# Graph network with four message layers: the collections' copies out of PSUM do part of the finishing, and statistics are taken by tile

## Chip, cores and metric

The program runs on one core of a Trainium2 chip. Its time is the device time of one execution in microseconds (us); of several executions the median is given.

## What is computed

Four message-passing layers (L = 0 to 3) run one after the other on 3125 nodes with 160 features each and 103125 edges. Each layer makes a message for each edge, sums the messages by target node, multiplies the sums by an output weight, finishes the row with node attribute, self-connection and gate, adds it to x and normalizes x over its 160 features. Cut to what the change touches (the sums over edges are `agg`, `scal`, `vec`, `ms`, `mv`):

```python
# layer 0
pre = self_connection + (agg @ lin2) * a * scale          # 192 columns
out = concat([silu(pre[:, :64]), sigmoid(pre[:, 64:96]) * pre_v])
# layer 1: returns x + attention output
# layer 2: mean over max(count, 1) edges
alpha = scal @ Wa * a * inv96
return sc + alpha * conv                                   # conv is also times a
# layer 3
angle = 0.1 * (ms @ W3) * a * inv96
return cos(angle) * sc + sin(angle) * (conv * a)
# after every layer
def _layernorm(x, axis=-1, eps=1e-05):
    m = jnp.mean(x, axis=axis, keepdims=True)
    v = jnp.var(x, axis=axis, keepdims=True)
    return (x - m) / jnp.sqrt(v + eps)
x = _layernorm(x + layer(x))
```

## The kernel before

Nodes are held in 25 tiles of 128 (n = `k.NT` = 25); `x` is one SBUF tile of 128 partitions by 25 by 160 numbers of 32 bits. Each layer is a row of phases, and each phase is a block in which every engine has its own program; between two phases all engines meet at a barrier (L139), so nothing of one phase overlaps the next. The phases of a layer are: `project` (rows of x times input weights, written to a table in memory), `messages` or the attention phases (most of the time, by groups of 512 edges), `collect`, and `finish`.

`collect` takes the sums per node (`acc`) and multiplies them by the output weight. For each of the 25 tiles TensorE (PE) transposes eight blocks of `acc` into `tp` (L430, L432), ScalarE (ACT) copies them to `st` and `st_rest` (L408 to L415), PE makes the product `po` with five matmuls (L442, L443), and VectorE (DVE) copies `po` out of PSUM to `out_all` (L468). `po` and `tp` have two slots each. PE starts the product of tile t+2 only when the copy of tile t is done (the semaphore `taken`, L439). In layer 1 DVE also divides `acc` by the softmax sums, one tile ahead of the transposes (L465), and PE waits for that (`scaled`, L428). The first two tiles and the last stand in straight code (in layer 1 the last three), the others in a loop that takes two tiles a round.

`hold` (L82) is a wait on a semaphore as an instruction of its own, which also counts up another semaphore. Inside the loop its value comes from a register, and so do the addresses `bass.ds(t, 1)`.

`finish` works on whole nodes, all 25 tiles in one instruction, 4000 numbers per partition: attribute and self-connection (L548, L549 in layer 0; L557, L558 in layer 1; L561 to L567 in layer 2; L570 to L594 in layer 3), then `layer_norm` (L485 to L493). Its instructions form a chain on DVE, each waiting for the one before (`link`). ACT is asked for silu, sigmoid, sine and square root (`ask`), each with a table load ahead of it. SP loads the next layer's input weights meanwhile (L270). `finish` ends before `project` starts.

Of the kernel before, what the change touches and what calls it, by code (L numbers as in the profile page):

```python
# [87 lines left out]
class Chain:  # L88
# [15 lines left out]
    def link(self, ins):  # L104
        self.need(self.run(ins))
# [268 lines left out]
                        v.sem_inc(drained)  # L374


def collect(nc, k, L, a, C, W, out_all, w, c):

    n = k.NT
    heads = L == 1  # L380
# [3 lines left out]
    with ExitStack() as scope:  # L384
# [9 lines left out]
        emptied = h.sem(name + "emptied")  # L394
        turned, staged, product, taken = (h.sem(name + "turned"), h.sem(name + "staged"), h.sem(name + "product"),
                                          h.sem(name + "taken"))
        with nc.Block() as block:

            @block.scalar
            def _(act):  # L400
                if not every:
                    act.wait_ge(emptied, 1)

                def step(t, s, i):
                    if not isinstance(t, int) or t >= 2:
                        hold(act, k, product, t - 1)
# [12 lines left out]
                rounds(act, n, step)  # L419

            @block.tensor
            def _(pe):
                def step(t, s, i):
                    if inside(t, n):
                        if not isinstance(t, int) or t >= 2:
                            pe.wait_ge(staged, t - 1)
                        if heads:
                            pe.wait_ge(scaled, t + 1)  # L428
                        for b in range(4):
                            pe.transpose(tp[:, s, 0, b * P:(b + 1) * P], acc[:, t * 4 + b, 0:P], k.ident[:, :])  # L430
                        for b in range(4):
                            mm = pe.transpose(tp[0:rest, s, 1, b * P:(b + 1) * P], acc[:, t * 4 + b, P:P + rest], k.ident[:, :])  # L432
                        mm.then_inc(turned, 1)
                    if inside(t - 1, n):
                        o = 1 - s
                        if isinstance(t, int) and t == 1:
                            pe.wait_ge(wready, 1)
                        if not isinstance(t, int) or t >= 3:
                            hold(pe, k, taken, t - 2)  # L439
                        pe.wait_ge(staged, t)  # L440
                        for y in range(4):
                            pe.matmul(po[:, o, 0:C], st[:, o, y, :, :].rearrange("p b n -> p (b n)"), w[:, y, :], start=y == 0, stop=False)  # L442
                        pe.matmul(po[:, o, 0:C], st_rest[:, o, :, :].rearrange("p b n -> p (b n)"), w[:, 4, :],  # L443
                                  start=False, stop=True).then_inc(product, 1)

                for t in range(n + 1):
                    step(t, t % 2, t // 2)

            @block.vector
            def _(v):  # L450
                chain = Chain(v, links)
                if not every:
                    chain.link(v.memset(st_rest[:, :, :, :], 0.0))
                    v.sem_inc(emptied)
                if heads:
                    chain.link(v.tensor_scalar(rden[:, :], acc[:, :, D], 1e-16, None, ALU.add))
                    chain.link(v.reciprocal(rden[:, :], rden[:, :]))
                else:
                    chain.link(v.tensor_tensor(w[:, :, :], w[:, :, :], c[:, :, :], ALU.mult))
                v.sem_inc(wready)  # L460

                def step(t, s, i):
                    if heads and inside(t + 2, n):
                        here = acc[:, bass.ds(t * 4 + 8, 4), 0:D]
                        v.tensor_tensor(here, here, over(rden[:, bass.ds(t * 4 + 8, 4)], 2, D), ALU.mult).then_inc(scaled, 1)  # L465
                    if inside(t, n):
                        hold(v, k, product, t + 1)
                        v.tensor_copy(out_all[:, bass.ds(t, 1), 0:C], po[:, s:s + 1, 0:C]).then_inc(taken, 1)  # L468

                rounds(v, n, step, before=2 if heads else 0)  # L470

# [7 lines left out]
    link(v.reciprocal(y, t))  # L479


def layer_norm(v, act_do, link, k, x, tmp, m, D_=D):

    n = x.shape[1]
    link(v.tensor_reduce(m[:, 0, :], x, AX.X, ALU.add))  # L485
    link(v.tensor_scalar(m[:, 0, :], m[:, 0, :], 1.0 / D_, None, ALU.mult))
    link(v.tensor_tensor(x, x, over(m[:, 0, :], 2, D_), ALU.subtract))  # L487
    link(v.tensor_tensor(tmp, x, x, ALU.mult))  # L488
    link(v.tensor_reduce(m[:, 1, :], tmp, AX.X, ALU.add))  # L489
    link(v.tensor_scalar(m[:, 1, :], m[:, 1, :], 1.0 / D_, EPS, ALU.mult, ALU.add))  # L490
    act_do()
# [4 lines left out]
def finish(nc, k, L, out_all, out, ahead):  # L496

    n = k.NT
    x = k.x
    with ExitStack() as scope:  # L500
# [17 lines left out]
        with nc.Block() as block:  # L518
# [17 lines left out]
            def _(v):  # L536
# [6 lines left out]
                    v.sem_inc(asked)  # L543
                    v.wait_ge(answered, count[0])

                at = over(k.attr[:, :], 2, D)
                if L == 0:
                    link(v.tensor_tensor(out_all[:, :, :], out_all[:, :, :], over(k.attr[:, :], 2, 2 * 96), ALU.mult))  # L548
                    link(v.tensor_tensor(out_all[:, :, :], out_all[:, :, :], k.sc[:, :, 0:192], ALU.add))  # L549
                    ask()  # L550
                    ask()
                    link(v.tensor_tensor(tmp[:, :, S:D].rearrange("p t (x c) -> p t x c", x=3),
                                         out_all[:, :, 96:192].rearrange("p t (x c) -> p t x c", x=3),
                                         over(out_all[:, :, S:S + V], 2, 3), ALU.mult))
                    link(v.tensor_tensor(x[:, :, :], x[:, :, :], tmp[:, :, :], ALU.add))
                elif L == 1:
                    link(v.tensor_tensor(x[:, :, :], x[:, :, :], x[:, :, :], ALU.add))  # L557
                    link(v.tensor_tensor(x[:, :, :], x[:, :, :], out_all[:, :, 0:D], ALU.add))  # L558
# [36 lines left out]
                layer_norm(v, ask, link, k, x[:, :, :], tmp[:, :, :], m)  # L595
                v.sem_inc(asked)


# [1068 lines left out]
def gnn_kernel(nc, a, out):  # L1667
    with ExitStack() as ctx:
# [39 lines left out]
        for L in range(4):  # L1708
            C = {0: 192, 1: D, 2: D + 2, 3: D + 1}[L]
            with ExitStack() as s2:  # L1710
# [12 lines left out]
                out_all = s2.enter_context(nc.sbuf_tensor(f"out_all{L}", [P, k.NT, C], F32))  # L1723
                collect(nc, k, L, a, C, D + 1 if L in (1, 2) else D, out_all, w, c)
# [3 lines left out]
                finish(nc, k, L, out_all, out if last else None, [] if last else following.loads)  # L1728
                if last:
                    break  # L1730
                if L == 0:
# [191 lines left out]
```

## Time and profile before

| | |
|---|---|
| median of 3 runs | 6664.72 us (6659.89 to 6674.17) |
| the profiled execution, its own time | 6672.04 us |
| its span, first to last instruction | 6670.3 us |
| busy, share of the span | PE 73%, DVE 73%, POOL 65%, ACT 31% |
| mean granted clock of TensorE | 0.877 |

The busy shares are means over phases that are limited in different ways; what a change in `collect` or `finish` is worth is read in the stretch of that phase. The chain of work that ended last reaches back only through the last `finish` phase, since a barrier stands ahead of it: each phase has a chain of its own. The four collections last some 60 us each and the four finishes some 32 to 45 us each, out of 6670.

### The profile page before, as it was taken

What the parts mean: (1) busy time and instruction counts of PE and PEld (TensorE: products, weight loads), DVE (VectorE), ACT (ScalarE), POOL (GpSimd) and SP (SyncE); (2) the same over time, 40 slices, a digit from 0 to 9 for tenths busy, and PEclk for the clock granted to TensorE, in tenths of its full rate; (3) what the DMA queues carried; (4) which work ended last, traced back from release to release, by engine and by line L of the source; (5) the groups of instructions that cost most, each with busy time, mean ns of one, the idle gap of its engine ahead of it and who ended that gap; (6) DMA issues with size and microseconds to landing.
All of it is one profiled execution on the core that took longest, in us unless ns stands there. A gap on an engine that the chain in (4) does not pass through costs nothing. (4 is left out here: it accounts for less than half of the span.)

```text
span 6670.3 us, 160444 instructions
## 1 busy us (share of the span) xinstructions
PE 4890.9 (73%) x45499; PEld 3804.3 (57%) x45500; DVE 4891.4 (73%) x10931; ACT 2090.6 (31%) x6090; POOL 4323.8 (65%) x4249
## 2 busy tenths in 40 slices
PE   5666667388888888888888577666766666687665
PEld 3444445277777777777777566544444454455444
DVE  5777775588888888888888744577777746666665
ACT  1000002166666666666666300300000011000011
POOL 5777775077767767777777155277777717777771
PEclk8888888699999999999999799888888888766787
DMA  3333332133333333333333166022222202222221
GB/s 106 88 88 89 89 89 66 40 91 94 91 91 91 90 91 91 91 90 90 93 91 91 54 184 186 27 71 70 70 70 70 72 28 68 67 67 67 67 67 34
DMA packets 401393, 545.13 MB, mean 82 GB/s; under 512 B 144934, under 2 KB 283318, under 8 KB 401180
## 3 DMA queue, kind: packets, MB, share of 16 engines
q0 software_dynamic: 193920, 331.22, 20.5%
q1 hardware_dynamic: 207388, 212.84, 11.3%
q8 instruction: 46, 0.75, 0.0%
q14 instruction: 39, 0.32, 0.0%
HBM read 464.79 MB, written 78.90 MB: 82 GB/s over the span
## 5 line engine op out<-in xcount | busy, mean ns | idle before, releaser
L763 POOL DMA_INDIRECT e_rows<-tab,e_idx x2424 | 2385.7, 984 | 808.8 <-issue 677.8
L1030 POOL DMA_INDIRECT acc<-tabx,a_idx x1616 | 1689.6, 1046 | 878.5 <-issue 467.0
L808 PE MATMUL e_wps<-e_w,e_hidT 64*128 64x192 f32 (+1 forms) x4848 | 803.2, 466 | 928.1 <-DVE e_hidT L877 927.2
L808 PEld LDWEIGHTS e_wps<-e_w,e_hidT 64*128 64x128 f32 x4848 | 547.1, 254 | 1137.8 <-DVE e_hidT L877 1020.7
L793 PE MATMUL e_win<-e_feat,e_ohy 128*32 128x96 f32 (+1 forms) x19392 | 1059.9, 338 | 25.1 <-DVE e_feat L871 25.0
L793 PEld LDWEIGHTS e_win<-e_feat,e_ohy 128*32 128x32 f32 x19392 | 724.7, 134 | 467.8 <-issue 322.0
L862 DVE TENSOR_TENSOR e_feat<-e_wps,e_rows 128x256 f32<-128x256 f32 x606 | 257.3, 425 | 922.5 <-DMA e_rows<-tab,e_idx 888.0
L871 DVE TENSOR_TENSOR e_feat<-e_wps,e_rows 128x384 f32<-128x384 f32 (+1 forms) x1616 | 720.0, 496 | 0.0
L1093 PE MATMUL a_c<-acc,a_buffer 128*128 128x64 f32 (+1 forms) x4848 | 624.8, 272 | 121.9 <-ACT a_buffer L1071 121.9
L1093 PEld LDWEIGHTS a_c<-acc,a_buffer 128*128 128x128 f32 (+1 forms) x4848 | 590.4, 192 | 144.0 <-issue 144.0
L782 ACT ACTIVATE e_idx<-src 128x4 int32 (+1 forms) x606 | 123.4, 205 | 1693.4 <-DMA e_rows<-tab,e_idx 1674.1
L1182 DVE TENSOR_TENSOR acc<-acc 128x1152 f32<-128x1152 f32 x404 | 545.5, 1350 | 0.0
L778 ACT ACTIVATE e_tanh<-e_hid 128x512 f32<-128x512 f32 x303 | 181.1, 598 | 1120.5 <-PE e_hid L814 1120.5
L1046 ACT ACTIVATE acc<-a_tps 128x512 f32<-128x512 f32 (+1 forms) x606 | 361.1, 596 | 389.9 <-PE a_tps L1089 389.8
L1071 ACT ACTIVATE a_buffer<-a_tps 128x512 f32<-128x512 f32 (+1 forms) x606 | 361.4, 596 | 381.2 <-PE a_tps L1089 371.1
L1089 PE MATMUL a_tps<-ident_sb,acc 128*128 128x128 f32 (+1 forms) x2424 | 377.5, 279 | 118.7 <-ACT acc L1046 105.7
L1093 PE MATMUL a_fv<-acc 128*128 128x64 f32 x3232 | 451.8, 262 | 0.0
L1093 PEld LDWEIGHTS a_fv<-acc 128*128 128x128 f32 x3232 | 451.1, 192 | 0.0
L1089 PE MATMUL a_tps<-ident_sb,a_buffer 128*128 128x128 f32 (+1 forms) x2424 | 377.4, 279 | 82.4 <-ACT a_buffer L1071 78.7
L1093 PE MATMUL a_scal<-acc 96*128 96x164 f32 x1616 | 376.9, 315 | 65.5 <-issue 45.6
L865 DVE TENSOR_TENSOR e_ohy<-e_oh,y 128x512 f32<-128x512 f32 x606 | 412.6, 681 | 0.0
L1548 POOL TENSOR_TENSOR s_ohx<-s_oh,ex 128x512 f32<-128x512 f32 x202 | 207.3, 1048 | 285.5 <-DVE s_oh L1611 285.5
(245 smaller groups left out, 7839.6 us busy)
## 6 DMA issues: line engine op xcount, KB each, us to landing
h_d<-a_buffer SPq DMA_DIRECT2D x202, 322.0 KB, 2.6
s_hin<-h_d SPq DMA_DIRECT2D x202, 322.0 KB, 3.2
e_rows<-tab,e_idx POOLq DMA_INDIRECT x2424
e_ein<-in_e64T SPq DMA_DIRECT2D x202, 128.0 KB
acc<-tabx,a_idx POOLq DMA_INDIRECT x1616
a_ein<-in_e_h SPq DMA_DIRECT2D x202, 64.0 KB
e_ein<-in_e16T SPq DMA_DIRECT2D x202, 32.0 KB
tab<-p_rows SPq DMA_DIRECT2D x36, 160.0 KB
```

Of the source, the lines that this page charges most:

```text
L763: pool.indirect_dma_start(out=rows[:, s, t, :], out_offset=None, in_=k.tab0, in_offset=bass.IndirectOffsetOnAxis(ap=idx[:, s, t:t + 1], ax ...
L793: mm = pe.matmul(win[NB * y:NB * (y + 1), s, 0:many * V], ohy[:, s, t, y, :], feat[:, s, t, first:first + (many - 1) * pitch + 1:pitch, :] ...
L808: mm = pe.matmul(wps[:, e, 2 * u + j, 0:WC], hidT[half, edges], w2[half, :], start=True, stop=True)
L862: v.tensor_tensor(f[:, :, slot("A0"):slot("A0") + 2, :], planar(w[:, :, 0:S]), planar(r[:, :, 0:S]), ALU.mult)
L865: v.tensor_tensor(ohy[:, e, :, :, :], over(oh[:, e, :, :], 2, 4), harmonics(g), ALU.mult)
L871: ins = v.tensor_tensor(f[:, :, slot(field):slot(field) + (many - 1) * pitch + 1:pitch, :], over(w[:, :, wc:wc + V], 2, many), planar(r[:, ...
L1030: pool.indirect_dma_start(out=rows[:, b, q, :], out_offset=None, in_=table, in_offset=bass.IndirectOffsetOnAxis(ap=idx[:, b, end, q:q + 1] ...
L1046: act.activation(featT[0:m, q, :], tps[0:m, :], ACT.Copy).then_inc(f_taken, 1)
L1071: act.activation(zT[0:m, q, :], tps[0:m, :], ACT.Copy).then_inc(z_taken, 1)
L1089: mm = pe.transpose(tps[0:m, q * P:(q + 1) * P], src[:, q, col:col + m], k.ident[:, :])
L1093: return pe.matmul(out, srcT[0:rows, j, q * P:(q + 1) * P], cw[key], start=True, stop=True)
L1182: return v.tensor_tensor(to[:, :, :, :, :].rearrange("p t j x c -> p t j (x c)"), over(of, 2, 3), y[:, :, 0:9].unsqueeze(3).to_broadcast([ ...
```

## The change

In `collect` the copy out of PSUM is replaced by an instruction or several that do the first steps of `finish` for that tile:

- layer 0: `po` times attribute plus self-connection, in one instruction, to `out_all`;
- layer 1: x becomes 2 x + `po` in one instruction, and BN_STATS writes six statistics of the tile's row of x (for the even and the odd elements: count, mean, and squared deviations summed) to `stats`;
- layer 2: four instructions on one element per partition make the factor from count, attribute and alpha; one multiplies `po` by it and adds the self-connection, one adds the result to x, and BN_STATS follows;
- layer 3: `po` times attribute in one instruction.

In `finish` the corresponding whole-node instructions are gone. In layers 1 and 2 `layer_norm` gets mean and variance from `stats` with seven instructions on 25 elements, and three passes over 4000 elements are gone; the subtraction of the mean stays. Layers 0 and 3 keep the old norm. `out_all` is there in layers 0 and 3 alone.

```diff
@@ collect, VectorE, for each tile
                     if inside(t, n):
                         hold(v, k, product, t + 1)
-                        v.tensor_copy(out_all[:, bass.ds(t, 1), 0:C], po[:, s:s + 1, 0:C]).then_inc(taken, 1)
+                        attr = k.attr[:, bass.ds(t, 1)]
+                        x = k.x[:, bass.ds(t, 1), :].rearrange("p o c -> p (o c)")
+                        old = k.sc[:, bass.ds(t, 1), :].rearrange("p o c -> p (o c)")
+                        if L == 0:
+                            row = out_all[:, bass.ds(t, 1), 0:C].rearrange("p o c -> p (o c)")
+                            v.scalar_tensor_tensor(row, po[:, s, 0:C], attr, old, ALU.mult, ALU.add).then_inc(taken, 1)
+                        elif L == 1:
+                            v.scalar_tensor_tensor(x, x, 2.0, po[:, s, 0:D], ALU.mult, ALU.add).then_inc(taken, 1)
+                            hold(v, k, taken, t + 1)
+                            v.bn_stats(stats[:, bass.ds(t, 1), :].rearrange("p o c -> p (o c)"), x)
+                        elif L == 2:
+                            count, each, both = (ratio[:, s, j:j + 1] for j in range(3))
+                            v.tensor_scalar(count, po[:, s, D + 1:D + 2], 1.0, None, ALU.max).then_inc(small, 1)
+                            hold(v, k, small, t * 4 + 1)
+                            v.reciprocal(count, count).then_inc(small, 1)
+                            hold(v, k, small, t * 4 + 2)
+                            v.tensor_tensor(each, count, attr, ALU.mult).then_inc(small, 1)
+                            hold(v, k, small, t * 4 + 3)
+                            v.scalar_tensor_tensor(both, po[:, s, D:D + 1], each, each, ALU.mult, ALU.mult).then_inc(small, 1)
+                            hold(v, k, small, t * 4 + 4)
+                            v.scalar_tensor_tensor(part[:, s, :], po[:, s, 0:D], both, old[:, 0:D], ALU.mult, ALU.add).then_inc(taken, 1)
+                            hold(v, k, taken, t + 1)
+                            v.tensor_tensor(x, x, part[:, s, :], ALU.add).then_inc(summed, 1)
+                            hold(v, k, summed, t + 1)
+                            v.bn_stats(stats[:, bass.ds(t, 1), :].rearrange("p o c -> p (o c)"), x)
+                        else:
+                            row = out_all[:, bass.ds(t, 1), 0:C].rearrange("p o c -> p (o c)")
+                            v.tensor_scalar(row, po[:, s, 0:C], attr, None, ALU.mult).then_inc(taken, 1)
@@ layer_norm
-    link(v.tensor_reduce(m[:, 0, :], x, AX.X, ALU.add))
-    link(v.tensor_scalar(m[:, 0, :], m[:, 0, :], 1.0 / D_, None, ALU.mult))
-    link(v.tensor_tensor(x, x, over(m[:, 0, :], 2, D_), ALU.subtract))
-    link(v.tensor_tensor(tmp, x, x, ALU.mult))
-    link(v.tensor_reduce(m[:, 1, :], tmp, AX.X, ALU.add))
+    if stats is None:
...
+    else:
+        link(v.tensor_tensor(m[:, 1, :], stats[:, :, 1], stats[:, :, 4], ALU.subtract))
+        link(v.tensor_tensor(m[:, 1, :], m[:, 1, :], m[:, 1, :], ALU.mult))
+        link(v.tensor_tensor(m[:, 2, :], stats[:, :, 2], stats[:, :, 5], ALU.add))
+        link(v.scalar_tensor_tensor(m[:, 1, :], m[:, 1, :], D_ / 4, m[:, 2, :], ALU.mult, ALU.add))
     link(v.tensor_scalar(m[:, 1, :], m[:, 1, :], 1.0 / D_, EPS, ALU.mult, ALU.add))
+    if stats is not None:
+        link(v.tensor_tensor(m[:, 0, :], stats[:, :, 1], stats[:, :, 4], ALU.add))
+        link(v.tensor_scalar(m[:, 0, :], m[:, 0, :], 0.5, None, ALU.mult))
+        link(v.tensor_tensor(x, x, over(m[:, 0, :], 2, D_), ALU.subtract))
@@ finish
                 if L == 0:
-                    link(v.tensor_tensor(out_all[:, :, :], out_all[:, :, :], over(k.attr[:, :], 2, 2 * 96), ALU.mult))
-                    link(v.tensor_tensor(out_all[:, :, :], out_all[:, :, :], k.sc[:, :, 0:192], ALU.add))
                     ask()
                     ask()
...
-                elif L == 1:
-                    link(v.tensor_tensor(x[:, :, :], x[:, :, :], x[:, :, :], ALU.add))
-                    link(v.tensor_tensor(x[:, :, :], x[:, :, :], out_all[:, :, 0:D], ALU.add))
-                elif L == 2:
...
-                    link(v.tensor_scalar(col[:, 0, :].unsqueeze(2), o[:, :, D + 1:D + 2], 1.0, None, ALU.max))
-                    link(v.reciprocal(col[:, 0, :], col[:, 0, :]))
-                    link(v.tensor_tensor(col[:, 0, :], col[:, 0, :], k.attr[:, :], ALU.mult))
-                    link(v.tensor_tensor(o[:, :, 0:D + 1], o[:, :, 0:D + 1], over(col[:, 0, :], 2, D + 1), ALU.mult))
-                    link(v.tensor_tensor(o[:, :, 0:D], o[:, :, 0:D], o[:, :, D:D + 1].to_broadcast([P, n, D]), ALU.mult))
-                    link(v.tensor_tensor(o[:, :, 0:D], o[:, :, 0:D], k.sc[:, :, 0:D], ALU.add))
-                    link(v.tensor_tensor(x[:, :, :], x[:, :, :], o[:, :, 0:D], ALU.add))
-                else:
-                    o = out_all
-                    link(v.tensor_tensor(o[:, :, 0:D + 1], o[:, :, 0:D + 1], over(k.attr[:, :], 2, D + 1), ALU.mult))
```

Layer 2's collection on DVE, before: the start of the loop's body. ISA and REGISTER_ALU rows are register arithmetic (an address or a wait's value); a wait stands in no row of this list.

```order
L71 ISA
L468 ISA
L468 COPY out_all<-c_po 128x162
L84 REGISTER_ALU
L468 ISA
L468 COPY out_all<-c_po 128x162
L71 REGISTER_ALU
```

The same place of the changed program, one tile of the two that a round of the loop takes (`c_ratio` is `ratio`, `c_part` is `part`, `keep` holds the self-connection):

```order
L482 TENSOR_SCALAR c_ratio<-c_po 128x1
L84 ISA
L484 RECIPROCAL c_ratio<-c_ratio 128x1
L84 REGISTER_ALU
L486 REGISTER_ALU
L486 TENSOR_TENSOR c_ratio<-c_ratio,attr 128x1
L84 REGISTER_ALU
L488 SCALAR_TENSOR_TENSOR c_ratio<-c_po,c_ratio 128x1
L84 REGISTER_ALU
L490 ISA
L490 SCALAR_TENSOR_TENSOR c_part<-c_po,c_ratio,keep 128x160
```

Where one copy stood, five instructions stand up to the one that frees `po`, and behind it the addition to x (L492) and BN_STATS (L494) each follow with a register row of their own ahead of them.

Layer 2's finish on DVE in the changed program, up to the subtraction of the mean; before, the thirteen instructions from L561 to L490 stood there, eight of them over 4000 elements:

```order
L521 TENSOR_TENSOR f_m<-stats 128x25
L522 TENSOR_TENSOR f_m<-f_m 128x25
L523 TENSOR_TENSOR f_m<-stats 128x25
L524 SCALAR_TENSOR_TENSOR f_m<-f_m 128x25
L525 TENSOR_SCALAR f_m<-f_m 128x25
L527 TENSOR_TENSOR f_m<-stats 128x25
L528 TENSOR_SCALAR f_m<-f_m 128x25
L529 TENSOR_TENSOR x<-x,f_m 128x4000
```

One pass over 4000 elements is left ahead of the square root, where before there were eight.

## Rows read from the trace of the kernel before

**Rows 1.** Windows, layer 2: stretch, length, five engines' busy time, PEclk, DMA, GB/s

```profile
5370.00:5380.00 10.00, 10.00 (x82) 10.00 (x80) 1.31 (x4) 3.69 (x10) 0.00 (x0) 1.00 0.00 0
...
5423.20:5466.00 42.80, 0.00 (x0) 0.00 (x0) 41.17 (x19) 1.51 (x2) 0.00 (x0) 0.55 0.05 15
```

**Rows 2.** Timeline, collection of layer 2: start, duration, engine, line, [idle before]

```profile
5369.54 0.33 DVE L468 COPY out_all<-c_po 128x162 f32<-128x162 f32 x1 [4.89 <-PE c_po L443]
...
5371.21 0.44 PE L443 MATMUL c_po<-c_w,c_st_rest 128*128 128x162 f32 x2
...
5375.72 0.44 PE L443 MATMUL c_po<-c_w,c_st_rest 128*128 128x162 f32 x2
...
5376.40 0.33 DVE L468 COPY out_all<-c_po 128x162 f32 x1 [1.93 <-PE c_po L443]
...
5422.77 0.33 DVE L468 COPY out_all<-c_po 128x162 f32<-128x162 f32 x1 [0.96 <-PE c_po L443]
```

**Rows 3.** Timeline, finish of layer 0

```profile
1191.70 1.28 ACT L512 ACT_TABLE_LOAD   x1 [3.17 <-PEq L139]
1191.74 5.16 DVE L548 TENSOR_TENSOR out_all<-out_all,attr 128x4800 f32<-128x4800 f32 x1 [0.75 <-PEq L139]
...
1202.18 1.54 ACT L512 ACTIVATE f_tmp<-out_all 128x1600 f32<-128x1600 f32 x1 [9.20 <-DVEq L543]
```

**Rows 4.** Timeline of DVE, finish of layer 1

```profile
4243.56 4.33 DVE L557 TENSOR_TENSOR x<-x 128x4000 f32<-128x4000 f32 x1 [1.12 <-PEq L139]
...
4256.63 0.18 DVE L486 TENSOR_SCALAR f_m<-f_m 128x25 f32<-128x25 f32 x1
4256.85 4.33 DVE L487 TENSOR_TENSOR x<-x,f_m 128x4000 f32<-128x4000 f32 x1
4261.20 4.32 DVE L488 TENSOR_TENSOR f_tmp<-x 128x4000 f32<-128x4000 f32 x1
...
4269.92 0.18 DVE L490 TENSOR_SCALAR f_m<-f_m 128x25 f32<-128x25 f32 x1
```

**Rows 5.** Timeline of DVE, finish of layer 2

```profile
5423.85 0.18 DVE L561 TENSOR_SCALAR f_col<-out_all 128x25 f32<-128x25 f32 x1 [0.76 <-PEq L139]
...
5459.75 0.18 DVE L490 TENSOR_SCALAR f_m<-f_m 128x25 f32<-128x25 f32 x1
```

**Rows 6.** Timeline of DVE, finish of layer 3

```profile
6611.95 4.35 DVE L570 TENSOR_TENSOR out_all<-out_all,attr 128x4025 f32<-128x4025 f32 x1 [0.76 <-PEq L139]
6616.34 0.18 DVE L574 COPY f_col<-out_all 128x25 f32<-128x25 f32 x1
```

**Rows 7.** Groups by line and form: count, busy us, mean ns

```profile
L849 DVE SCALAR_TENSOR_TENSOR acc<-e_win,lo,acc 128x160 f32 x404 | 150.9, 374 | 4.0 <-PE e_win L793 4.0
...
L1362 DVE TENSOR_TENSOR_SCAN acc<-acc 101x1024 f32<-101x1024 f32 x8 | 18.3, 2291 | 0.3
...
L475 DVE RECIPROCAL f_m<-f_m 128x25 f32<-128x25 f32 x4 | 1.3, 316 | 1.4 <-ACT f_m L517 1.4
```

**Rows 8.** Timeline of DVE, attention: the second waits for the first by one hold

```profile
2503.05 0.54 DVE L1249 TENSOR_TENSOR a_buffer<-a_c,acc 128x384 f32<-128x384 f32 x1
2503.74 0.55 DVE L1253 TENSOR_TENSOR a_buffer<-a_buffer,a_c 128x384 f32<-128x384 f32 x1
```

**Rows 9.** Timeline of DVE, collection of layer 1, one round of the loop

```profile
4193.37 0.33 DVE L468 COPY out_all<-c_po 128x160 f32 x1 [1.17 <-PE c_po L443]
4193.63 0.83 DVE L465 TENSOR_TENSOR acc<-acc,c_rden  x1
4195.60 0.33 DVE L468 COPY out_all<-c_po 128x160 f32 x1 [1.14 <-PE c_po L443]
4196.14 0.83 DVE L465 TENSOR_TENSOR acc<-acc,c_rden  x1 [0.21 <-issue]
```

**Rows 10.** Windows, start of layer 1's finish, columns as in rows 1

```profile
4245.00:4247.00 2.00, 0.00 (x0) 0.00 (x0) 2.00 (x1) 0.00 (x0) 0.00 (x0) 0.79 0.87 257
```

**Rows 11.** Windows, messages of layer 0, columns as in rows 1

```profile
920.00:925.00 5.00, 1.72 (x38) 1.30 (x28) 4.19 (x11) 0.58 (x2) 3.78 (x5) 1.00 0.43 111
```

More of the change, by code:

```diff
@@ L374, in _, with collect @@
                         v.sem_inc(drained)
-def collect(nc, k, L, a, C, W, out_all, w, c):
+def collect(nc, k, L, a, C, W, out_all, stats, w, c):
     n = k.NT
@@ L393, in collect @@
         links, scaled, wready = h.sem(name + "links"), h.sem(name + "scaled"), h.sem(name + "wready")
-        emptied = h.sem(name + "emptied")
+        ratio = h.sb(name + "ratio", [P, 2, 3]) if L == 2 else None
+        part = h.sb(name + "part", [P, 2, D]) if L == 2 else None
+        emptied, small, summed = h.sem(name + "emptied"), h.sem(name + "small"), h.sem(name + "summed")
         turned, staged, product, taken = (h.sem(name + "turned"), h.sem(name + "staged"), h.sem(name + "product"),
@@ L479, in inverse_root, with layer_norm @@
     link(v.reciprocal(y, t))
-def layer_norm(v, act_do, link, k, x, tmp, m, D_=D):
+def layer_norm(v, act_do, link, k, x, tmp, m, stats=None, D_=D):
     n = x.shape[1]
-    link(v.tensor_reduce(m[:, 0, :], x, AX.X, ALU.add))
-    link(v.tensor_scalar(m[:, 0, :], m[:, 0, :], 1.0 / D_, None, ALU.mult))
-    link(v.tensor_tensor(x, x, over(m[:, 0, :], 2, D_), ALU.subtract))
-    link(v.tensor_tensor(tmp, x, x, ALU.mult))
-    link(v.tensor_reduce(m[:, 1, :], tmp, AX.X, ALU.add))
+    if stats is None:
+        link(v.tensor_reduce(m[:, 0, :], x, AX.X, ALU.add))
+        link(v.tensor_scalar(m[:, 0, :], m[:, 0, :], 1.0 / D_, None, ALU.mult))
+        link(v.tensor_tensor(x, x, over(m[:, 0, :], 2, D_), ALU.subtract))
+        link(v.tensor_tensor(tmp, x, x, ALU.mult))
+        link(v.tensor_reduce(m[:, 1, :], tmp, AX.X, ALU.add))
+    else:
[3 more added lines that the diff above has]
+        link(v.scalar_tensor_tensor(m[:, 1, :], m[:, 1, :], D_ / 4, m[:, 2, :], ALU.mult, ALU.add))
     link(v.tensor_scalar(m[:, 1, :], m[:, 1, :], 1.0 / D_, EPS, ALU.mult, ALU.add))
+    if stats is not None:
+        link(v.tensor_tensor(m[:, 0, :], stats[:, :, 1], stats[:, :, 4], ALU.add))
+        link(v.tensor_scalar(m[:, 0, :], m[:, 0, :], 0.5, None, ALU.mult))
+        link(v.tensor_tensor(x, x, over(m[:, 0, :], 2, D_), ALU.subtract))
     act_do()
@@ L493, in layer_norm, with finish @@
     link(v.tensor_tensor(x, x, over(m[:, 2, :], 2, D_), ALU.mult))
-def finish(nc, k, L, out_all, out, ahead):
+def finish(nc, k, L, out_all, stats, out, ahead):
     n = k.NT
@@ L544, in ask @@
                     v.wait_ge(answered, count[0])
-                at = over(k.attr[:, :], 2, D)
                 if L == 0:
-                    link(v.tensor_tensor(out_all[:, :, :], out_all[:, :, :], over(k.attr[:, :], 2, 2 * 96), ALU.mult))
-                    link(v.tensor_tensor(out_all[:, :, :], out_all[:, :, :], k.sc[:, :, 0:192], ALU.add))
                     ask()
@@ L555, in _ @@
                     link(v.tensor_tensor(x[:, :, :], x[:, :, :], tmp[:, :, :], ALU.add))
-                elif L == 1:
-                    link(v.tensor_tensor(x[:, :, :], x[:, :, :], x[:, :, :], ALU.add))
-                    link(v.tensor_tensor(x[:, :, :], x[:, :, :], out_all[:, :, 0:D], ALU.add))
-                elif L == 2:
+                elif L == 3:
                     o = out_all
-                    link(v.tensor_scalar(col[:, 0, :].unsqueeze(2), o[:, :, D + 1:D + 2], 1.0, None, ALU.max))
-                    link(v.reciprocal(col[:, 0, :], col[:, 0, :]))
-                    link(v.tensor_tensor(col[:, 0, :], col[:, 0, :], k.attr[:, :], ALU.mult))
-                    link(v.tensor_tensor(o[:, :, 0:D + 1], o[:, :, 0:D + 1], over(col[:, 0, :], 2, D + 1), ALU.mult))
-                    link(v.tensor_tensor(o[:, :, 0:D], o[:, :, 0:D], o[:, :, D:D + 1].to_broadcast([P, n, D]), ALU.mult))
-                    link(v.tensor_tensor(o[:, :, 0:D], o[:, :, 0:D], k.sc[:, :, 0:D], ALU.add))
-                    link(v.tensor_tensor(x[:, :, :], x[:, :, :], o[:, :, 0:D], ALU.add))
-                else:
-                    o = out_all
-                    link(v.tensor_tensor(o[:, :, 0:D + 1], o[:, :, 0:D + 1], over(k.attr[:, :], 2, D + 1), ALU.mult))
                     angle = o[:, :, D:D + 1]
@@ L594, in _ @@
                     link(v.tensor_tensor(x[:, :, :], x[:, :, :], o[:, :, 0:D], ALU.add))
-                layer_norm(v, ask, link, k, x[:, :, :], tmp[:, :, :], m)
+                layer_norm(v, ask, link, k, x[:, :, :], tmp[:, :, :], m, stats)
                 v.sem_inc(asked)
@@ L1722, in gnn_kernel @@
                     messages(nc, k, L, a, a[eT], RW, WC, count, scale, ahead)
-                out_all = s2.enter_context(nc.sbuf_tensor(f"out_all{L}", [P, k.NT, C], F32))
-                collect(nc, k, L, a, C, D + 1 if L in (1, 2) else D, out_all, w, c)
+                wide = L in (0, 3)
+                out_all = s2.enter_context(nc.sbuf_tensor(f"out_all{L}", [P, k.NT, C], F32)) if wide else None
+                stats = None if wide else s2.enter_context(nc.sbuf_tensor(f"stats{L}", [P, k.NT, 6], F32))
+                collect(nc, k, L, a, C, D + 1 if L in (1, 2) else D, out_all, stats, w, c)
                 last = L == LAST
@@ L1727, in gnn_kernel @@
                 following = None if last else InputWeights(nc, s2, L + 1, width, a)
-                finish(nc, k, L, out_all, out if last else None, [] if last else following.loads)
+                finish(nc, k, L, out_all, stats, out if last else None, [] if last else following.loads)
                 if last:
```

## The prediction

> **What bounds the kernel now.** I read the chain of waits first. It reaches back only through the last finish phase and is DVE from end to end there; barriers cut the rest, so I took the windows of each collection and finish by themselves. The reader is to see two opposite phases. In layer 2's collection PE is busy 10.00 of 10.00 us at a granted clock of 1.00 and DVE only 1.31 us; in its finish DVE is busy 41.17 of 42.80 us and PE not at all [rows 1]. So a collection ends when PE does and a finish when DVE's chain does, and DVE work taken out of a finish and put into a collection costs nothing as long as PE stays the slower. How much room there is shows in the collection's timeline: PE's last product matmuls of two tiles stand 4.51 us apart over two tiles, 2.26 us a tile, and DVE idles 1.93 us ahead of its copy of 0.33 us [rows 2].
>
> **What is taken out of the finishes.**
>
> Layer 0: two passes over 4800 numbers. The chain then goes on with ACT's silu at 1202.18. Its table load ran beneath the passes, from 1191.70 to 1192.98 [rows 3], and is bare once they are gone; silu can start at 1192.98, not at 1191.74. Gain 1202.18 - 1192.98 = 9.20 us.
>
> Layer 1: what stood from the first instruction to the end of L490 took 4270.10 - 4243.56 = 26.54 us. In its place come seven instructions on 25 elements and the subtraction of the mean. From start to start a small one takes 0.22 us and a full pass 4.35 [rows 4], so 7 x 0.22 + 4.35 = 5.89. Gain 20.65 us. ACT's table load (1.28 us as in layer 0) stays hidden beneath 5.89.
>
> Layer 2: 5459.93 - 5423.85 = 36.08 us [rows 5] become 5.89. Gain 30.19 us.
>
> Layer 3: one pass over 4025 numbers, 6616.34 - 6611.95 = 4.39 us [rows 6].
>
> Together 64.4 us. What was hidden beneath the finishes is SP's load of the next weights: in layer 1 it is at its height 1.5 to 3.5 us after the finish begins (257 GB/s) [rows 10], and a finish of some 12 us still covers it.
>
> **What is put into the collections.** The prices of DVE instructions: 25 elements take 0.18 us and 4000 take 4.33 [rows 4], so 1.04 ns an element and 0.15 to 0.16 us fixed. The scalar-tensor-tensor with a scalar per partition takes 0.374 us for 160 columns [rows 7], 0.04 more than the copy; for one element 0.374 - 0.167 = 0.21. A reciprocal of 25 elements takes 0.316 [rows 7]; for one element it lies between 0.16 and 0.32 and I take 0.17, since the excess should go with the elements. BN_STATS occurs nowhere. The cheap bound is an element a step, 0.33 us as the copy; the dear one the scan, 2.29 us for 1024 [rows 7], which is 2.13 ns an element and 0.49 us. I take 0.33, as a pass that writes six numbers is nearer to a reduction than to a scan.
>
> Layers 0 and 3: one instruction for one, 0.05 us longer, in DVE's 1.9 us of idle time; only the last tile's counts, +0.05 each.
>
> Layer 1: scalar-tensor-tensor, hold, BN_STATS, and the division for a later tile. What a wait costs here decides the rest. In straight order, one hold between an instruction and one that needs it: 2503.74 - (2503.05 + 0.54) = 0.15 us [rows 8]. Where an address is worked out in registers behind the hold: 5376.40 - (5375.72 + 0.44) = 0.24 us [rows 2]. From one instruction to an independent one: starts 0.26 us apart, 0.54 where the loop's branch lies between [rows 9]. So from the start of the scalar-tensor-tensor BN_STATS starts at 0.37 + 0.24 = 0.61, the division at 0.87 or 1.15, and ends at 1.70 or 1.98. The copy's start is 0.24 behind the product, so the division is done 1.94 or 2.22 us behind product t; PE wants it after product t+1, 2.23 us later [rows 9]. It fits by 0.3 or by a hair; I add 0.3 us in all for the hair. The last tile adds 0.04 + 0.15 + 0.33 = 0.52. Layer 1: -20.65 + 0.82 = -19.8 us.
>
> Layer 2 is where the cover runs out. Per tile: 0.16 + 0.17 + 0.16 + 0.21 + 0.37 + 0.33 + 0.33 = 1.73 us of instructions, less than PE's 2.26. But each needs the one before. Six waits lie between: two followed at once by the instruction (0.15 each, ahead of L484 and L488) and four with a register row behind them (0.24 each, ahead of L486, L490, L492, L494): 1.26 us. To the next tile the engine goes at -0.07 (0.26 - 0.33) or, past the branch, at +0.21, on average +0.07. That is 3.06 us a tile against PE's 2.26: DVE becomes the bound of this collection, and PE waits on `taken`. In straight code the gaps are 6 x 0.15 = 0.90. Sum: 2 x 2.56 + 22 x 3.06 + 2.63 = 75.1 us from the first instruction on `po` to the last one's end. Before, 5423.10 - 5369.54 = 53.6 [rows 2]. Layer 2's collection grows by 21.5 us, and the layer gains 30.2 - 21.5 = 8.7 us.
>
> A rule speaks against counting waits at all. The row shows 0.15 us behind one wait, 0.24 with an address [rows 2, 8]. The Trainium skill ("VectorE: DVE Perf Modes", The DRAIN you can't avoid) says that a semaphore after each instruction costs nothing extra over a chain without. By it a tile would take 1.73 us, PE would stay the bound and layer 2 would keep nearly all of its 30 us; by the rows it keeps 8.7. I go by the rows, because that measurement had no waits as instructions of their own. The same page (The TRN2 errata) warns that many small tiles each pay the fixed time, with (N+151)/0.96 ns for an fp32 tensor-tensor, 157 ns before the first element. The fixed 0.15 to 0.16 us of the rows agrees, and it is in the sum.
>
> **The sum.** Layer 0 -9.15, layer 1 -19.8, layer 2 -8.7, layer 3 -4.35: -42.0 us. The profiled execution took 6672.0 us, so 6630.0; it lies 7.3 us above the median of the runs shown, 6664.7, from which the same difference gives 6622.7. I say 6623. With BN_STATS at 0.49 layer 2 loses 4.0 more and every second tile of layer 1 0.14 more, 1.5 together: -36.5, 6628. With shorter gaps behind register rows (0.20 in place of 0.24) layer 2 gets back 88 x 0.04 = 3.5: 6619. The forecast's own range, with the runs' scatter of some 5 us, is 6612 to 6634.
>
> **Rivals.**
>
> A: the waits overlap with the instructions and PE stays layer 2's bound. For it: DVE idles 1.93 us a tile and the new instructions add only 1.4. Against it: the 0.15 and 0.24 us are bare gaps between dependent work. Only the last tile's tail, some 2 us, would be added: -64.4 + 0.1 + 0.8 + 2 = -61.5, 6603 us. Chance 0.09.
>
> B: PE, now held up by DVE for 0.8 us of each 3.06, falls to the lower of its two clocks (1.2 GHz) for part of layer 2's collection. A tile would then take up to 2 x 2.26 = 4.5 us. For half of the tiles that is 12 x 1.45 = 18 us: 6641. Against it: in the messages PE is busy 1.72 of 5 us and has 1.00 of the clock granted [rows 11]. With it go longer gaps than I read. Chance 0.10.
>
> C, the other side: BN_STATS is slow. Layer 1's DVE round is 1.3 us and its length, so PE stays the bound up to 0.94 us and each 0.1 more costs 2.5 us there and 2.5 in layer 2. The gain of 42.0 is used up where 25 (b - 0.33) + 25 (b - 0.94) = 42, b = 1.48 us, 9 ns an element; at 1.6 us the time would be 6671. The dearest operation of the rows, the reciprocal, has 0.14 us over the plain 25 elements, 5.4 ns an element [rows 7]. Chance 0.03.
>
> D: the gains are made elsewhere up again, say by less of PE's clock in the phases behind, and nothing is left. PE stands still for the whole of each finish either way (its clock there is 0.55 on average [rows 1]). Chance 0.02.
>
> The forecast itself has 0.76. The range from 6610 to 6642 holds the forecast and B and leaves A, C and D out. A measurement of this kernel tells 0.2%, 13 us, from no change. Faster by more than that are the forecast, A and B: 0.95; within it D: 0.02; slower C: 0.03.
>
> **What would show it.** In layer 2's collection the starts of BN_STATS stand 2.9 and 3.2 us apart in turn, DVE has no wait on PE, and PE waits on DVE's L490 some 0.8 us a tile; A shows 2.26 us apart and DVE idle. In layer 1 the period stays 2.23 to 2.26. BN_STATS shows 0.33 us (0.49 if dear). Silu starts 1.3 us after the barrier. The finishes' chains before the root are 5.9 us long. I would be wrong most of all by the six gaps: each 0.05 us on all of them is 6 x 25 x 0.05 = 7.5 us.

## The result and the profile after

The changed kernel takes 6623.43 us (median of 6 executions, 6619.84 to 6626.2) against 6666.64 us of the kernel before (6 executions of the same set), a ratio of 0.9934 with a 95% interval of 0.9922 to 0.9947. It is 43.2 us faster; the forecast was 42.0 us and 6623 us. Its profiled execution took 6621.51 us, span 6619.7 us.

All phases end at a barrier, so the difference can be read phase by phase. Windows of the changed kernel for the collections and finishes of layers 0 to 3 (columns as in [rows 1]; each stretch goes from barrier to barrier, to 0.1 us):

```profile
1121.70:1189.20 67.50, 66.01 (x450) 62.95 (x450) 11.60 (x26) 38.47 (x125) 0.00 (x0) 0.95 0.00 1
1189.20:1226.00 36.80, 0.00 (x0) 0.00 (x0) 30.14 (x14) 6.48 (x6) 0.00 (x0) 0.55 0.03 9
...
4165.40:4230.70 65.30, 60.57 (x450) 56.12 (x450) 36.69 (x77) 38.48 (x125) 0.00 (x0) 0.95 0.00 1
4230.70:4243.90 13.20, 0.00 (x0) 0.00 (x0) 11.17 (x14) 1.51 (x2) 0.00 (x0) 0.64 0.17 50
...
5327.90:5408.20 80.30, 63.69 (x450) 58.48 (x450) 43.45 (x177) 18.77 (x50) 0.00 (x0) 0.97 0.00 1
5408.20:5421.10 12.90, 0.00 (x0) 0.00 (x0) 11.17 (x14) 1.51 (x2) 0.00 (x0) 0.51 0.18 51
...
6504.80:6565.40 60.60, 59.16 (x450) 57.31 (x450) 10.90 (x27) 18.63 (x50) 0.00 (x0) 0.95 0.00 1
6565.40:6619.40 54.00, 0.00 (x0) 0.00 (x0) 42.98 (x30) 3.24 (x5) 0.00 (x0) 0.53 0.12 38
```

The same eight stretches of the kernel before:

```profile
1124.30:1191.30 67.00, 65.53 (x450) 62.47 (x450) 10.10 (x26) 38.55 (x125) 0.00 (x0) 0.96 0.00 1
1191.30:1237.30 46.00, 0.00 (x0) 0.00 (x0) 40.45 (x16) 6.48 (x6) 0.00 (x0) 0.54 0.02 7
...
4179.70:4242.80 63.10, 59.33 (x450) 56.83 (x450) 28.61 (x52) 38.55 (x125) 0.00 (x0) 0.95 0.00 1
4242.80:4276.60 33.80, 0.00 (x0) 0.00 (x0) 31.80 (x14) 1.51 (x2) 0.00 (x0) 0.55 0.07 20
...
5362.60:5423.40 60.80, 59.48 (x450) 58.98 (x450) 9.44 (x27) 18.80 (x50) 0.00 (x0) 0.95 0.01 1
5423.40:5466.40 43.00, 0.00 (x0) 0.00 (x0) 41.17 (x19) 1.51 (x2) 0.00 (x0) 0.54 0.05 15
...
6551.30:6611.50 60.20, 58.94 (x450) 57.10 (x450) 9.42 (x27) 18.63 (x50) 0.00 (x0) 0.95 0.00 1
6611.50:6670.00 58.50, 0.00 (x0) 0.00 (x0) 47.33 (x31) 3.24 (x5) 0.00 (x0) 0.53 0.11 35
```

With the barriers' own times (the DRAIN of DVE at L139, to 0.01 us) the differences are: layer 0 +0.5 and -9.2, layer 1 +2.3 and -20.6, layer 2 +19.6 and -30.2, layer 3 +0.3 and -4.4 us, together -41.7. The phases that the change does not touch came out 8.9 us shorter in this pair of profiles; they scatter by some us from one execution to the next, and the message phases most of all. These windows also show the finishes before as 46.0, 33.8, 43.0 and 58.5 us; the last is longer than the 32 to 45 us given ahead of the prediction.

The greatest loss is layer 2's collection. Timeline of DVE there, the changed kernel, a tile and the start of the next two (to be set beside [rows 2]):

```profile
5342.06 0.33 DVE L494 BATCH_NORM_STATS2 stats<-x  x1 [0.24 <-DVE x L492]
5342.31 0.14 DVE L482 TENSOR_SCALAR c_ratio<-c_po 128x1 f32<-128x1 f32 x1
5342.60 0.16 DVE L484 RECIPROCAL c_ratio<-c_ratio 128x1 f32<-128x1 f32 x1
5342.98 0.16 DVE L486 TENSOR_TENSOR c_ratio<-c_ratio,attr 128x1 f32<-128x1 f32 x1 [0.22 <-DVE c_ratio L484]
5343.28 0.22 DVE L488 SCALAR_TENSOR_TENSOR c_ratio<-c_po,c_ratio 128x1 f32<-128x1 f32 x1
5343.74 0.38 DVE L490 SCALAR_TENSOR_TENSOR c_part<-c_po,c_ratio,keep 128x160 f32<-128x160 f32 x1 [0.24 <-DVE c_ratio L488]
5344.36 0.32 DVE L492 TENSOR_TENSOR x<-x,c_part 128x160 f32 x1 [0.24 <-DVE c_part L490]
5344.93 0.33 DVE L494 BATCH_NORM_STATS2 stats<-x  x1 [0.24 <-DVE x L492]
5345.44 0.16 DVE L482 TENSOR_SCALAR c_ratio<-c_po 128x1 f32<-128x1 f32 x1 [0.19 <-issue]
...
5348.08 0.33 DVE L494 BATCH_NORM_STATS2 stats<-x  x1 [0.24 <-DVE x L492]
```

BN_STATS starts 2.87 and 3.15 us apart in turn (5342.06, 5344.93, 5348.08), 3.01 a tile against TensorE's 2.26 before. No gap is a wait for PE. Four of them, 0.22 to 0.24 us, stand where a register row follows the wait; the bare waits leave 0.15 (5342.31 + 0.14 to 5342.60). It is PE that waits, for the instruction that frees `po` (from the list of waits in this phase: us in total, times, longest):

```profile
PE c_po L444 <- DVE c_part L490: 11.0, 20, 1.5
```

That is 0.55 us in each of 20 tiles. The engines' busy time in that phase is far from showing this: DVE 43.45 of 80.30 us, PE 63.69.

### The profile page after: what moved, and what is told of

Its sections match the earlier page's. It is cut to its first block and busy times, and to the rows that moved or that the text cites. A ratio compares the mean times of both kernels' runs of the same rounds, so it can differ in the third digit from the quotient of the medians.

```text
span 6619.7 us, 160960 instructions
## 1 busy us (share of the span) xinstructions
PE 4893.9 (74%) x45499; PEld 3808.5 (58%) x45500; DVE 4875.7 (74%) x11098; ACT 2088.4 (32%) x6090; POOL 4319.6 (65%) x4249
## 3 DMA queue, kind: packets, MB, share of 16 engines
q0 software_dynamic: 193920, 331.22, 20.6%
## 5 line engine op out<-in xcount | busy, mean ns | idle before, releaser
L1052 POOL DMA_INDIRECT acc<-tabx,a_idx x1616 | 1690.6, 1046 | 867.3 <-issue 467.9
L1570 POOL TENSOR_TENSOR s_ohx<-s_oh,ex 128x512 f32<-128x512 f32 x202 | 207.1, 1046 | 283.9 <-DVE s_oh L1633 283.9
```

Of the source, the lines that this page charges most:

```text
L1052: pool.indirect_dma_start(out=rows[:, b, q, :], out_offset=None, in_=table, in_offset=bass.IndirectOffsetOnAxis(ap=idx[:, b, end, q:q + 1] ...
```

## The experiments

Unless it says otherwise, the layer named in an experiment is the only one that differs from the changed kernel. Phase times stand in windows as above; whole times are set against the kernel before, run beside them. The kernel before took 6652.94 us beside the first four experiments and 6666.64 beside the first result, so their whole times are compared as differences, not with the times in us that the expectations name.

**Layer 2 undone.** `collect` copies `po` again in layer 2 and `finish` does the rest.

```diff
                         elif L == 2:
-                            count, each, both = (ratio[:, s, j:j + 1] for j in range(3))
...
-                            v.bn_stats(stats[:, bass.ds(t, 1), :].rearrange("p o c -> p (o c)"), x)
+                            v.tensor_copy(out_all[:, bass.ds(t, 1), 0:C], po[:, s:s + 1, 0:C]).then_inc(taken, 1)
```

> Layer 2 as before the change, the other layers changed. Theory (layer 2's collection is held up by chains of waits on VectorE and gives back two thirds of what its finish gains): layer 2's collection falls from 80.4 to 60.8 us and its finish rises from 12.8 to 43.0, so the time is 10.6 us above the changed kernel's, 6634 us. Rival (the whole gain of layer 2's finish is used up again): the time is that of the changed kernel within 3 us.

The collection and the finish of layer 2:

```profile
5324.70:5385.20 60.50, 59.18 (x450) 58.71 (x450) 9.44 (x27) 18.77 (x50) 0.00 (x0) 0.95 0.00 1
5385.20:5428.20 43.00, 0.00 (x0) 0.00 (x0) 41.17 (x19) 1.51 (x2) 0.00 (x0) 0.54 0.05 15
```

6623.68 us against 6652.94 of the kernel before: 29.3 us below, where the changed kernel, in another set, stands 42.7 us below. Layer 2's part of the change is a gain, of 10.3 us by the phases (80.4 + 12.8 against 60.5 + 43.0) and some 13 us by the medians of the two sets. The rival falls.

**Layer 2's loop written out, waits kept.**

```diff
-                rounds(v, n, step, before=2 if heads else 0)
+                rounds(v, n, step, before=2 if heads else 0, lo=n if L == 2 else 2)
```

> Layer 2's VectorE loop written out, so that waits and addresses are constants; the six waits between dependent instructions stay instructions of their own. Theory (waits as instructions cost 0.15 us, register rows behind them 0.09 more, the branch 0.28 a round): a tile takes 2.56 in place of 3.02 us, and layer 2's collection 80.4 - 22 x 0.46 = 70.3 us. Rival (the number of instructions and their fixed time bound it): 80.4 us as in the changed kernel.

```profile
5326.30:5396.90 70.60, 63.17 (x450) 58.27 (x450) 42.28 (x177) 18.76 (x50) 0.00 (x0) 0.96 0.00 1
```

70.6 us, with the same 177 DVE instructions as in the changed kernel. A tile's timeline has all gaps at 0.15 us; from one L482 to the next it is 2.51 us (5345.10 to 5347.61). Three single gaps in the phase are 0.50 to 0.53 us; their cause is open. The registers and the branch were 9.8 us. Whole time 6605.87 us, 47.1 below the kernel before, where the changed kernel's 43.2 and these 9.8 would make 53; the whole times scatter by some us and do not bear the phase's gain out in full.

**The same with plain waits.** In addition to the loop written out, for all six waits inside a tile:

```diff
-                            hold(v, k, small, t * 4 + 1)
+                            v.wait_ge(small, t * 4 + 1)
```

> Layer 2's VectorE loop written out and the waits inside a tile plain, so that each goes with the instruction behind it. Theory: gaps fall to 0.03 us, the chain of a tile to 1.9 us, below TensorE's 2.26; TensorE bounds the collection again, at 60.8 us and 1.6 us for the last tile's tail, 62.4, and the time is 18 us below the changed kernel's, 6605 us. Rival (instruction count and fixed time): 80.4 us, time unchanged.

Windows of the phase, and the start of its list of waits:

```profile
5322.30:5385.00 62.70, 59.32 (x450) 58.82 (x450) 44.53 (x177) 18.77 (x50) 0.00 (x0) 0.95 0.01 1
...
ACT c_st L410 <- PE c_tp L434: 57.6, 25, 21.1
DVE c_ratio L482 <- PE c_po L445: 11.9, 23, 4.7
```

62.7 us. DVE does the same 177 instructions and waits for PE at 23 tiles; the timeline shows 0.03 us between dependent instructions and 2.26 us between tiles. 6593.74 us, ratio 0.9911 (0.9897 to 0.9924), 59.2 us below the kernel before, where the 43.2 of the changed kernel and the 18 expected here would make 61. So it is neither the count of instructions nor their fixed time, but the waits between them. `hold` waits and counts up in one instruction, and the plain wait goes with the next one; no run tells whether the extra instruction costs the time or its counting up, and none has plain waits inside the loop.

**Waits doubled.** Each of the six `hold` lines stands twice. In the set of this run, of "Both together", of the first run with BN_STATS in all finishes and of the first repeat of the changed kernel, TensorE was granted a mean clock of 0.686, and the kernel before took 9566.17 us; the message and attention phases are longer there, while finishes and collections last as long as elsewhere (80.38 us for layer 2's collection in the first profile of the changed kernel, 79.4 here). These runs are read by their phases.

> The changed kernel with each of layer 2's six waits between dependent instructions given twice; the second is met when it is reached. Theory (a wait as an instruction costs its 0.11 us in a chain with nothing to cover it): 6 x 0.11 = 0.66 us more a tile, layer 2's collection 80.4 + 16.5 = 97 us. Rival (a wait that is met costs nothing): 80.4 us.

```profile
7731.50:7830.00 98.50, 63.12 (x450) 57.48 (x450) 43.48 (x177) 18.80 (x50) 0.00 (x0) 0.97 0.00 1
```

98.5 us, 18 to 19 more than once each. Its timeline, with the wait doubled ahead of a bare instruction and ahead of one with a register row:

```profile
7751.67 0.16 DVE L485 RECIPROCAL c_ratio<-c_ratio 128x1 f32<-128x1 f32 x1 [0.26 <-DVE c_ratio L482]
7752.16 0.16 DVE L488 TENSOR_TENSOR c_ratio<-c_ratio,attr 128x1 f32<-128x1 f32 x1 [0.33 <-DVE c_ratio L485]
```

0.26 in place of 0.15 and 0.33 in place of 0.22: a wait instruction that is met already adds 0.11 us here, 16.5 us for 150 of them. The remaining 2.6 of the 19.1 us in this set are longer turns at the branch (0.27 to 0.33 in place of 0.18 us) and a few single gaps.

**Layer 1's statistics one tile later.** BN_STATS of tile t-1 stands behind the division of `acc` for tile t+2.

```diff
+                    if heads and inside(t - 1, n):
+                        hold(v, k, taken, t)
+                        v.bn_stats(stats[:, bass.ds(t - 1, 1), :].rearrange("p o c -> p (o c)"),
+                                   k.x[:, bass.ds(t - 1, 1), :].rearrange("p o c -> p (o c)"))
...
                             v.scalar_tensor_tensor(x, x, 2.0, po[:, s, 0:D], ALU.mult, ALU.add).then_inc(taken, 1)
-                            hold(v, k, taken, t + 1)
-                            v.bn_stats(stats[:, bass.ds(t, 1), :].rearrange("p o c -> p (o c)"), x)
...
-                rounds(v, n, step, before=2 if heads else 0)
+                rounds(v, n, step, before=2 if heads else 0, after=1 if heads else 0)
```

> Layer 1's statistics of a tile are taken one tile later, behind the next division of acc. Theory (in every second tile the division comes too late for the weight load of TensorE's transposes by some 0.2 us): layer 1's collection falls from 65.4 to 63.7 us (63.1 before the change, plus the last tile's tail of 0.5). Rival (the longer collection comes of the slower instruction that frees the product): 65.4 us as in the changed kernel.

Rows of the list of waits in layer 1's collection, first of the changed kernel:

```profile
PEld c_tp L432 <- DVE acc L467: 5.4, 1, 5.4
...
DVE stats L479 <- DVE x L477: 4.8, 20, 0.2
PEld c_tp L432 <- issue: 2.5, 9, 0.3
```

and the window of the experiment:

```profile
4161.90:4225.20 63.30, 59.04 (x450) 56.55 (x450) 34.82 (x77) 38.55 (x125) 0.00 (x0) 0.95 0.01 1
```

63.3 us, 2.1 less than 65.4. The nine pauses of TensorE's weight load (PEld) ahead of the transposes, 2.5 us, are gone. The list puts them down to "issue", that is to nothing it can see; that they were waits for the division is read from the times and borne out by this run. One of them in the changed kernel: the division L467 ends at 4182.71, and the weight load of L432 starts at 4182.83, 0.47 us behind the start of the product L445 at 4182.36; in an undisturbed tile it is 0.13 us (4178.02 behind 4177.89). The rival falls. The one execution, 6615.87 us, is 37.1 below the kernel before; it says nothing of 2 us.

**Both together.**

> Layer 1's statistics a tile later and layer 2's VectorE loop written out with plain waits, together. Theory: the two gains add, 17.7 + 2.1 = 19.8 us below the changed kernel. Rival (layer 1's order matters only by chance of the clock): 17.7 us.

Layer 1's and layer 2's collections, in the set with the low clock:

```profile
6156.60:6219.20 62.60, 58.32 (x450) 55.83 (x450) 34.82 (x77) 38.56 (x125) 0.00 (x0) 0.95 0.00 1
...
7797.90:7859.30 61.40, 58.01 (x450) 57.57 (x450) 44.60 (x177) 18.80 (x50) 0.00 (x0) 0.97 0.01 1
```

2.9 and 18.0 us less than the changed kernel of that set (65.5 and 79.4). The whole times of that set, 9491.17 us against the changed kernel's 9493.67, cannot tell 20 us: each scatters by 37 to 80 us. By the phases both gains are there together; the whole time does not show them.

**Statistics by BN_STATS in all finishes, and silu's table early.** On top of both:

```diff
                 rounds(act, n, step)
+                if L == 0:
+                    act.activation(early[:, :], k.ones[:, 0:1], ACT.Silu)
...
+                if stats is None:
+                    for t in range(n):
+                        chain.run(v.bn_stats(own[:, t, :], x[:, t, :]))
+                    chain.need(chain.at)
```

> On top of e5_both: in the finishes of layers 0 and 3 too the statistics come from BN_STATS, 25 instructions of 160 columns one behind the other without waits, in place of three passes over 4000, and ScalarE loads silu's table at the end of layer 0's collection. Theory: instructions without waits start 0.25 us apart, so 6.3 + 1.5 + 4.4 = 12.2 us stand in place of 17.9, 5.7 less in each of the two finishes, and silu starts 1.2 us sooner: 12.6 us below e5_both. Rival (many small instructions cost more than few large ones, as fixed time is paid 25 times): 25 x 0.33 = 8.2 us in place of 6.3 and a gain of at most 3.8 us a finish, 8.8 in all.

> e8_more again. By its phases (layer 0's finish 29.5 us, layer 3's 47.9, the collections of layers 1 and 2 63 and 61 us) it should be 33 to 35 us below the changed kernel and 75 us below the kernel before, ratio 0.9887. Rival (the phases' gains do not add up in the whole time): less than 25 us below the changed kernel.

The second run, finishes of layers 0 and 3, and the group of the new instructions in layer 0:

```profile
1185.10:1214.50 29.40, 0.00 (x0) 0.00 (x0) 23.91 (x41) 5.19 (x5) 0.00 (x0) 0.56 0.04 11
...
6534.30:6582.20 47.90, 0.00 (x0) 0.00 (x0) 36.74 (x57) 3.24 (x5) 0.00 (x0) 0.53 0.14 43
...
L625 DVE BATCH_NORM_STATS2 f_own<-x 128x6 f32<-128x160 f32 x25 | 5.8, 310 | 0.0
```

The two finishes fall by 7.4 and 6.1 us, 0.5 more each than expected: 25 instructions without waits overlap and are busy 5.8 us together, where each alone takes 0.31. The whole time does not follow as far: 6591.55 us, 20.7 below the changed kernel of its set, where the edited phases add up to 34.1. As far as the whole time goes, the rival of the second expectation holds. The profiled execution, 6584.35 us, is the fastest of the four and 27.9 below the changed kernel's profiled one; in it phases that no edit touches were longer (attention 4.8, the sums behind it 2.6, one `project` 2.6 us). The other three are 6 to 11 us slower still, and no trace shows where. The sums behind the attention took 372.2 us in both profiles of this kernel and 369.6 to 370.3 in those of all the others, so that part is no scatter; its cause is open. The first run of this kernel, in the low-clock set, took 9476.7 us, 17 below the changed kernel, and says no more.

**Subtraction and root in one pass.** On top of that:

```diff
-        link(v.tensor_tensor(x, x, over(m[:, 0, :], 2, D_), ALU.subtract))
...
-    link(v.tensor_tensor(x, x, over(m[:, 2, :], 2, D_), ALU.mult))
+    for t in range(n):
+        chain.run(v.tensor_scalar(x[:, t, :], x[:, t, :], m[:, 3, t:t + 1], m[:, 2, t:t + 1], ALU.subtract, ALU.mult))
+    chain.need(chain.at)
```

> On top of e8: in all four norms the subtraction of the mean and the multiplication with the inverse root, two passes over 4000 numbers, become 25 instructions of 160 columns that do both, with two scalars per partition. Theory (independent instructions start at their length less 0.08 us, 0.30 us apart if they cost 0.38 as the one with a scalar per partition on PSUM does, 0.25 if as the copy): 6.3 to 7.5 us in place of 8.7, 1.2 to 2.4 less in each norm, 5 to 10 us below e8. Rival (two scalars per partition make each of them slower than 0.43 us): no gain or a loss.

```profile
5373.60 6.91 DVE L537 TENSOR_SCALAR x<-x,f_m 128x160 f32<-128x160 f32 x25
```

6.91 us for what took 2 x 4.35; each finish is 1.8 us shorter. 6576.34 us, ratio to the kernel before 0.9885 (0.987 to 0.99), 36 us below the changed kernel of its set, where the edited phases add up to 41.4. It is the fastest version. It stands 15.2 us below the kernel of the step before, more than the 5 to 10 expected and twice the 7.1 that the four finishes give; the difference between those two whole times is therefore not the price of this edit, and the phases are what shows it.

**The changed kernel again**, twice, for these comparisons.

> The changed kernel once more, beside the kernel before on one chip, so that the other kernels can be set against it. Theory: by its phases it is 41.7 us below the kernel before, ratio 0.9937. Rival (the phases that the change does not touch also gained, as they did by 8.9 us in the first profile): 50 us, ratio 0.9925.

> The changed kernel once more, so that the two kernels below can be set against it on one chip. Theory: 41.7 us below the kernel before by its phases, ratio 0.9937 where an execution takes 6.65 ms; rival 50 us, ratio 0.9925.

In the last set the changed kernel takes 6612.29 against 6655.01 us, 42.7 below, ratio 0.9935 (0.9922 to 0.9949). The ratios of theory and rival, 0.9937 and 0.9925, both lie in this interval; the differences of 43.2 and 42.7 us in the two sets at the usual clock are nearer to 41.7 than to 50. In the set with the low clock it is 72.5 us below, ratio 0.9931 (0.9907 to 0.9955). The ratios of the expectation hold for an execution of 6.65 ms; of 9566 us, 41.7 would be 0.9956 and 50 would be 0.9948. That set is nearer to the rival, but its message and attention phases move by tens of us from one execution to the next, and it decides nothing.

## Why the prediction was right

**The finishes** came out to a tenth: -9.2, -20.6, -30.2, -4.4 us against 9.20, 20.65, 30.19 and 4.39. Silu starts at 1190.95, right behind a table load that runs from 1189.65 to 1190.93, as the step on layer 0 had it; that is 1.7 us after the barrier and not the 1.3 given as a sign, as the load itself begins 0.4 after it.

**Layer 2's collection** was priced at +21.5 us and grew by 19.6. The sum of a tile's instructions (1.73 us) measured 1.74, the gaps (1.26) 1.23, the turn to the next tile (0.07) 0.04, and a tile 3.00 over the loop where 3.06 was forecast: 1.3 of the 1.9 us. The first product also stood 0.5 us nearer to the barrier than before (5334.28 behind 5327.86, against 5369.54 behind 5362.62). PE's wait on L490 is 0.55 us a tile where 0.8 was given; its weight load pauses 0.8 (15.7 us in 20). The cause is shown, not only timed: with the same instructions and shorter gaps the phase falls to 70.6 and 62.7 us, with more waits it grows to 98.5. The prediction's reason for going by the rows, that the measurement told in the Trainium skill had no waits as instructions of their own, is not stated there; the choice rested on the rows alone.

**Layer 1's collection** is the term that was mis-sized by a step of its own: +0.8 us forecast, +2.3 measured (+2.6 in the last set). The step "I add 0.3 us in all for the hair" looked at when TensorE's transposes begin. What needs the divided `acc` is their weight load, which starts about 0.3 us ahead of the end of the product; so in nine of the tiles the division came 0.3 us late, not by a hair. The period did not stay at 2.23 to 2.26 us: L477 starts at 4180.80, 4183.05 and 4185.53, 2.25 and 2.48 us apart. Moving the statistics took 2.1 us back.

**Luck.** The sum fits the phases by 0.3 us because errors cancel: layer 2's collection 1.9 us less than forecast, layer 1's 1.4 more, those of layers 0 and 3 0.5 and 0.3 where 0.05 each was forecast (in the last set they were 0.5 and 1.1 below the kernel before, so these two are scatter). That the median met 6623 to 0.4 us is closer than one execution is to the next.

**BN_STATS** costs 0.327 us for 160 columns, the cheap bound. The scalar-tensor-tensor of layer 2 took 0.383 where 0.374 was taken, layer 1's, with a number in place of a scalar per partition, 0.322. The dear bound was (2.29 - 0.15) / 1024 = 2.09 ns an element and not 2.13; its 0.49 us stays.

**The rivals.** A (waits hidden) was wrong for the changed kernel and right for the one with plain waits. Here the Trainium skill ("VectorE: DVE Perf Modes", The DRAIN you can't avoid) and the trace part by what a wait is: joined to the next instruction it left 0.03 us, close to nothing as that section says; as an instruction of its own it left 0.15, and with a register row behind it 0.22 to 0.24. B (a lower clock of PE) did not occur: in all of layer 2's collection from 5340 to 5400 the granted clock is 1.00, though PE stood still for a tenth to a fifth of it. Two of its stretches:

```profile
5340.00:5350.00 10.00, 9.01 (x69) 8.26 (x67) 5.64 (x24) 2.60 (x9) 0.00 (x0) 1.00 0.00 0
5350.00:5360.00 10.00, 8.04 (x58) 7.35 (x59) 5.58 (x23) 2.95 (x8) 0.00 (x0) 1.00 0.01 2
```

C (slow BN_STATS) is off the table at 0.327 us. D did not occur: the whole time fell by 43.2 us.

That the untouched phases gave nothing is argued, not shown: layer 0's messages, the same code in all kernels, took 1046 to 1053 us in the eight profiles at the usual clock of kernels with the change, but 1056.6 in the one profile of the kernel before. That execution took 6672.04 us, 5.4 above its median, and the changed kernel's profiled one is 1.9 below its own; that is 7.3 of the 8.9 us.

## What to carry to other kernels

Work moved beneath a slower engine is free only as long as the chain of one round, with its waits, is shorter than that engine's round; add up the gaps, not only the instructions. Between dependent small instructions on VectorE the form of the wait decided: joined to the instruction 0.03 us, alone 0.15, with a register row behind it 0.22 to 0.24. A register that only gives the wait its value cost nothing: ahead of L484 and L488 the gap is 0.15 in the loop and in straight code alike. When something is taken out of a chain of large passes, look for what their length had covered, such as a table load; and where TensorE loads an operand as weights, as it does `acc` here, it must be ready for the weight load, which began 0.3 us ahead of the end of the matmuls in front of it.

## What the runs showed that I had not expected

Twenty-five independent instructions of 160 columns are dearer than one pass over 4000, but by less than their lengths add up to. BN_STATS starts every 0.23 us, 25 of them take 5.8 us (25 x 0.33 would be 8.2), and one pass over 4000 takes 4.33; a tensor-scalar with two scalars per partition, 25 times, takes 6.91. They pay here because each does the work of several passes: 5.8 us replace three passes (13.1 us) and 6.91 replace two (8.7).

In one set the kernel before took 9566 us in place of 6653, with a mean granted clock of 0.686. Layer 0's messages of the changed kernel took 1554 us there in place of 1053:

```profile
67.60:1621.70 1554.10, 972.10 (x8282) 521.52 (x8282) 794.55 (x2122) 84.67 (x303) 796.33 (x808) 0.72 0.23 61
...
68.40:1121.70 1053.30, 715.39 (x8282) 443.73 (x8282) 787.52 (x2122) 100.21 (x303) 796.50 (x808) 0.83 0.36 89
```

TensorE was busy 972 us for the same matmuls in place of 715, VectorE and GpSimd as long as before within 1%. The collections kept their length at a granted clock of 0.97. The first four experiments had run on the same chip at the usual clock (0.86 to 0.89). Why the clock fell later was not tried, and that the clock alone makes the phases longer is not shown.
